# Rank and bias products in fp16, first expert rows ahead of three weight loads, row indices in a ring

## The chip, the cores and the metric

One core of a Trainium2 chip. The metric is the device time of one execution in microseconds (us), the median of the runs. The core has a matrix engine (PE), a vector engine (DVE), an activation engine (ACT), a general engine (POOL) and a queue engine (SP). Transfers are issued from SP, ACT and POOL. PE's clock is granted at one of two levels, 1.2 and 2.4 GHz; the profile shows it as 0.50 and 1.00.

## The reference

The input is `x` (32 sequences of 64 tokens, 256 features, float32). Four layers follow each other:

```python
# L0: adapter with one of 16 domain experts per sequence, residual, layer norm
hidden = gelu(x @ down_W.T + down_b)
hidden = hidden @ expert_W[idx].T + expert_b[idx] + domain_emb[idx]
x = layernorm(hidden @ up_W.T + up_b + x) * gamma + beta
# L1: attention (16 heads, bias and mask) with adaptive norm, then a feed-forward of 1024
# L2: rotation of feature pairs by theta and phi of the sequence
# L3: norms, a style per sequence, then a mixture of 8 experts, two per token
probs = softmax(h_flat @ router_w)
gates, idx = top_k(probs, 2)
gates = gates / gates.sum(-1, keepdims=True)
combine = zeros((N, 8)).at[arange(N)[:, None], idx].add(gates)
hid = relu(einsum('nd,edf->nef', h_flat, exp_w1) + exp_b1)
eout = einsum('nef,efd->ned', hid, exp_w2) + exp_b2
y = einsum('ned,ne->nd', eout, combine)
return x + y
```

## The kernel before, in words

The 2048 tokens go in four chunks of 512 through layers 0 to 2 and the routing of layer 3. The order of every engine's work is written out by hand, and semaphores join the engines. Chunk `c` of the second half overlaps with the first half of later chunks. Each chunk holds 4 groups (TT) of 128 tokens.

The routing of a chunk: `route` (PE, L1573) makes the logits, `choose` (DVE, L1119) finds the two experts and writes `picks`, `rank` (PE, L1588) multiplies `picks` by a triangular matrix `lower` and by `ones` to give each token its place among the tokens of its expert, `token_gates` (DVE, L1140) works out the two gates, `find_place` (DVE, L1128) turns ranks into row numbers, and `dispatch` (POOL, L565) scatters each token's row twice to `dispatched` in device memory, in a region per expert. A row holds the features as fp16 halves (high and low), the token's number, its first expert and its gate values. `confirm` (POOL, L577) waits until the scatter has landed and tells ACT (`rows_sent`).

The expert biases are added by token, apart from the experts: `turn_gates` (PE, L1599) transposes the gate matrix, `copy_gates` (DVE, L1165) copies it from PSUM to `gate_f`, `expert_biases` (PE, L1605) multiplies it by `moe_b2`, `accumulate` (DVE, L1169) adds the result to the residual stream as `x4b`, and `store` (ACT's queue, L740) writes it to the output and counts `x_stored`. In chunks 0 to 2, DVE's order is `choose`, `token_gates`, `find_place`, `copy_gates`, `fill_rows` (the low halves of the rows), `split_low` (the split of the expert weights into fp16 halves, L910; SP loads the next part into `stage` after it), norm2, `accumulate`. In the last chunk it is `choose`, `token_gates`, `fill_rows`, `find_place`, the plan of the expert loop (L1318 to L1345, which tile of 128 rows belongs to which expert), `copy_gates`, `accumulate`.

The expert loop handles 39 tiles of 128 rows, sorted by expert. The split weights of all 8 experts come from `w_split` to `w_moe` in SBUF, 2048 KB each: experts 0 to 4 early, experts 5 to 7 (L491) only once `x_stored` says that the last store has landed, since they lie over buffers of the chunks. On ACT's queue, after `store` and the loads of the plan's values to registers (L812), `load_rows` (L816) loads the rows of a tile into `xs`; tiles 0 and 1 first, each later tile as a buffer gets free. PE turns the rows (`turn_rows`, L1707), DVE copies them to `xs_f` and works out the gates of the tile (`rows_in`, L1353). A step on PE is the up products of tile n mixed with the down products of tile n-2, with the turn of the rows of tile n+1 in its middle. ACT applies the bias and relu (L825), DVE splits the result in halves (L1377), ACT and DVE scale the output (L835, L1371) into `ys`, and POOL adds it to the output by an indirect transfer with the tile's row numbers `ids` (`add_rows`, L620), one at a time.

Of the kernel before, what the change touches and what calls it, by code (L numbers as in the profile page):

```python
# [25 lines left out]
P = 128  # L26
# [6 lines left out]
E = 8  # L33
# [36 lines left out]
        ("sty_b1", SH // 2, 1), ("sty_b2", P, 2 * KD), ("moe_b1", P, E * KF), ("iota_e", P, E),  # L70
        ("iota_t", P, ENTRIES), ("tile_m", P, NT), ("region", P, E))

# [12 lines left out]
def build(nc, t, out):  # L85
    with ExitStack() as ctx:
# [82 lines left out]
        moe_b1 = col["moe_b1"].rearrange("p (e f) -> p e f", e=E)  # L169
        iota_e, iota_t, tile_m, region = (col[n] for n in ("iota_e", "iota_t", "tile_m", "region"))  # L170
        ints = sb("ints", [P, 3 * B + NT], I32)
        dom_i, time_i, sub_i, tok_id = (ints[:, 0:B], ints[:, B:2 * B], ints[:, 2 * B:3 * B], ints[:, 3 * B:])
# [10 lines left out]
        router = sb("router", [P, KD, E])  # L183
        moe_b2 = sb("moe_b2", [E, D])
        mask_u8 = sb("mask_u8", [P, NT, S], U8)
# [57 lines left out]
        gate = sb("gate", [P, TT, E])  # L243
        gate_f = sb("gate_f", [E, CT])

        ones = sb("ones", [P, P])
        first1 = first
        first2 = sb("first2", [P, TT])
        picks = sb("picks", [P, TT + 1, E])
        seen = sb("seen", [P, E])  # L250
# [36 lines left out]
        ident16 = sb("ident16", [P, P], F16)  # L287
        meta = sb("meta", [P, ENTRIES, 4])
        gates = sb("gates", [P, ENTRIES])
# [7 lines left out]
        ys_low = [x1_kept[:, j, D:2 * D] for j in range(2)]  # L297
        ids = [sb(f"ids{j}", [P, 1], U32) for j in range(2)]
        xs_dram = nc.dram_tensor("dispatched", (E * CAP + P, ROW), F32).ap()
# [43 lines left out]
        h3_ready = count("h3_ready", 1)  # L343
        logit_done, gap_ready, gap_exp = count("logit_done", 1), count("gap_ready", 1), count("gap_exp", 1)
        gate_ready, gate_turned, gate_f_ready = count("gate_ready", 1), count("gate_turned", 1), count("gate_f_ready", 1)
# [3 lines left out]
        second_step = count("second_step", 58)  # L349

# [41 lines left out]
        def _(sp):  # L392
# [96 lines left out]

            sp.wait_ge(x_stored.sem, x_stored.of(NCH, 0))  # L490
            load_weights(FIRST_HALF, E)  # L491
            sp.wait_ge(weights_in, 16 * E)
# [3 lines left out]
        def _(pool):  # L496
# [122 lines left out]

            def add_rows(n, j):  # L620


                pool.wait_ge(gates_ready, n + 1)
                pool.nop(nofuse=True)
                pool.tensor_copy(ids[j][:], meta[:, bass.ds(n, 1), 0].bitcast(U32)).then_inc(ids_ready, 1)  # L625
                pool.wait_ge(ids_ready, n + 1)
                pool.wait_ge(ys_ready, n + 3)
                pool.nop(nofuse=True)
                pool.indirect_dma_start(  # L629
                    out=out[:, :], out_offset=bass.IndirectOffsetOnAxis(ap=ids[j][:, 0:1], axis=0),  # L630
                    in_=ys[j], in_offset=None, bounds_check=N - 1, oob_is_err=False,
                    compute_op=ALU.add).then_inc(rows_out, 16)
                pool.wait_ge(rows_out, n * 16 + 16)
                pool.nop(nofuse=True)
                pool.sem_inc(added, 1)

            pool.sem_inc(added, 2)
            with pool.Fori(0, TILES // 2) as i:
                for j in range(2):
                    add_rows(i * 2 + j, j)  # L640
            if TILES % 2:
                add_rows(TILES - 1, 0)

# [234 lines left out]
        def _(dve):  # L878
# [17 lines left out]
            dve.wait_ge(early_in, N_EARLY)  # L896
            dve.tensor_copy(ident16[:], ident[:]).then_inc(zeroed, 1)
            dve.tensor_copy(next_row[:], region[:]).then_inc(zeroed, 1)
            step(dve.tensor_copy(dom_f[:], dom_i[:]))
# [8 lines left out]
            assert done[0] == SETUP_DOM  # L908
            dve.wait_ge(zeroed, 8)
            def split_low(c, q):  # L910
# [130 lines left out]
            def second_half(c):  # L1041
# [98 lines left out]
                def token_gates():  # L1140

                    dve.wait_ge(rows_sent.sem, rows_sent.of(c, 0))
                    dve.tensor_copy(disp[:, :, D].bitcast(I32), tok_id[:, bass.ds(c * TT, TT)])
                    dve.tensor_scalar(disp[:, :, D + 1], first1[:], 100.0, None, ALU.add)
                    dve.wait_ge(gap_exp.sem, gap_exp.of(c, 1))
                    vec(dve.tensor_scalar(gate_d[:], gap_e[:], 1.0, None, ALU.add))
                    vec(dve.reciprocal(gate1[:], gate_d[:]))
                    vec(dve.tensor_tensor(gate2[:], gap_e[:], gate1[:], ALU.mult))

                    vec(dve.tensor_scalar(disp[:, :, D + 2], gate2[:], 1.0 / W_SCALE, None, ALU.mult))  # L1150
                    dve.scalar_tensor_tensor(disp[:, :, D + 3], gate1[:], 1.0 / W_SCALE, disp[:, :, D + 2], ALU.mult,
                                             ALU.subtract).then_inc(disp_ready.sem, 1)
                    dve.tensor_tensor(gated1[:], hot1[:], wide(gate1), ALU.mult)
                    vec(dve.tensor_tensor(gated2[:], hot2[:], wide(gate2), ALU.mult))
                    dve.tensor_tensor(gate[:], gated1[:], gated2[:], ALU.add).then_inc(gate_ready.sem, 1)

# [20 lines left out]

# [174 lines left out]

            def rows_in(n, j):  # L1353
# [8 lines left out]
                dve.wait_ge(gate_step, n * 2 + 2)  # L1362
                dve.tensor_tensor(gates[:, bass.ds(n, 1)], gates[:, bass.ds(n, 1)], xs[j][:, D + 2:D + 3],
# [17 lines left out]

            dve.sem_inc(ys_ready, 2)
            rows_in(0, 0)
            rows_in(1, 1)
            for g in range(2):
                halves(0, 0, 0, g)
            rows_in(2, 0)
            for g in range(2):
                halves(1, 1, 1, g)
            with dve.Fori(0, TURNS) as i:  # L1390
                for j in range(STEPS):
                    rows_in(i * STEPS + j + 3, (j + 1) % 2)
                    halves(i * STEPS + j + 2, j % 2, (j + 2) % 3, 0)
                    outputs(i * STEPS + j, j % 2)
                    halves(i * STEPS + j + 2, j % 2, (j + 2) % 3, 1)
            for n in range(LEFT, TILES):
                rows_in(n + 1, (n + 1) % 2)
                halves(n, n % 2, n % 3, 0)
# [7 lines left out]
        def _(pe):  # L1406
# [198 lines left out]
            def expert_biases(c):  # L1605
                pe.wait_ge(gate_f_ready.sem, gate_f_ready.of(c, 1))
# [26 lines left out]
            domain_experts(0)  # L1633
            pe.wait_ge(zeroed, 8)
            up_projection(0)
# [229 lines left out]
```

## Time and profile before

| what | value |
|---|---|
| median of 3 runs | 761.92 us (759.7 to 762.53) |
| the profiled execution | 761.58 us |
| its span in the trace | 759.8 us |
| busy PE / DVE / POOL / ACT | 577.8 / 481.5 / 281.6 / 262.7 us |
| mean granted clock of PE | 0.857 |

The profile is of one execution. The span goes from its first to its last instruction; 1.8 us lie around it. A busy share is an average over stages with different limits, so the stages are read one by one. The chunks take the time to about 494 us, the passage to the expert loop lies from there to 511 us, the loop itself ends near 741 us.

### The profile page before, as it was taken

The page shows a single profiled execution, that of the slowest core. Times are in us where ns is not written, and L with a number is a line of the kernel's source. Part 1 is how long each engine was busy: PE and PEld are TensorE (multiplying, and loading weights), DVE is VectorE, ACT ScalarE, POOL GpSimd, SP SyncE. Part 2 cuts the span into 40 slices and gives each one's busy share as a digit, 9 for nine tenths or more (in the row PEclk, how much of TensorE's full clock was granted, in tenths as well). Part 3 has the DMA queues.
Part 4 walks back from the last instruction along what each step waited for, and adds up shares of the span by engine and source line. Part 5 has one row for each costly group of instructions (what it writes and reads, how often), then busy time and mean ns, then how long its engine had stood idle before and what let it go on. Part 6 is the DMA issues. An engine that isn't in the chain of part 4 may idle for free.

```text
span 759.8 us, 16208 instructions
## 1 busy us (share of the span) xinstructions
PE 577.8 (76%) x5068; PEld 433.1 (57%) x5069; DVE 481.5 (63%) x1306; ACT 262.7 (35%) x548; POOL 281.6 (37%) x200
## 2 busy tenths in 40 slices
PE   3528678995969978589384871439999999999992
PEld 1415375583754747438383361327777787777771
DVE  5674784899679996717966127714656565655661
ACT  1215534524344153243231401004444444444440
POOL 0831628077055480564705010300423333323332
PEclk9558599998888999779785795559999999999997
DMA  8622474133064321553205673256223222222220
GB/s 291 234 78 66 145 251 141 34 112 110 2 227 190 102 82 40 177 239 112 102 9 166 230 278 137 97 192 227 44 40 47 44 42 42 44 41 36 49 42 1
DMA packets 41144, 86.28 MB, mean 114 GB/s; under 512 B 7317, under 2 KB 31790, under 8 KB 37006
## 3 DMA queue, kind: packets, MB, share of 16 engines
q1 hardware_dynamic: 22896, 65.13, 24.5%
q0 software_dynamic: 7200, 8.60, 6.6%
q10 hardware_dynamic: 11006, 12.01, 5.3%
q8 instruction: 25, 0.41, 0.2%
q14 instruction: 17, 0.14, 0.1%
HBM read 57.18 MB, written 29.44 MB: 114 GB/s over the span
## 4 chain that ended last, share of the span: by engine, by line
PE 55%; DVE 21%; DMA 8%; issue 5%; ACT 3%; POOL 3%; ACTq 3%; POOLq 0%; SPq 0%; DVEq 0%
PE bank L1563 8%; PE bank L1732 7%; PE bank L1554 6%; PE bank L1721 4%; PE bank L1723 4%; PE bank L1722 4%; DMA out_x<-x_kept,ids 4%; DMA stage<-in_moe_w 4%; PE bank L1733 3%; PE bank L1451 2%; PE bank L1518 2%; PE bank L1534 2%; PE bank L1508 2%; DVE split L914 2%; PE bank L1490 2%
## 5 line engine op out<-in xcount | busy, mean ns | idle before, releaser
L1721 PE MATMUL bank<-xs_f,w_moe 128*128 128x128 f16 x624 | 124.1, 221 | 6.9 <-issue 5.5
L1723 PE MATMUL bank<-xs_f,w_moe 128*128 128x128 f16 x624 | 124.1, 221 | 0.0
L1722 PE MATMUL bank<-xs_f,w_moe 128*128 128x128 f16 x624 | 123.6, 221 | 0.0
L825 ACT ACTIVATE stage<-bank,cols 128x128 f32<-128x128 f32 x312 | 88.5, 377 | 95.9 <-PE bank L1723 83.2
L629 POOL DMA_INDIRECT out_x<-x_kept,ids x39 | 61.9, 1587 | 65.0 <-DVE x_kept L1371 34.9
L1721 PEld LDWEIGHTS bank<-xs_f,w_moe 128*128 x624 | 61.4, 98 | 43.1 <-issue 14.1
L1732 PE MATMUL bank<-w_moe,split 128*128 x208 | 78.7, 380 | 0.7
L573 POOL DMA_INDIRECT dispatched<-disp,slot x32 | 34.1, 1067 | 121.0 <-DVE disp L1160 56.7
L1554 PE MATMUL bank<-w_moe 128*128 128x512 f32 x128 | 63.1, 656 | 16.2 <-ACT w_moe L707 16.2
L1416 PE MATMUL bank<-mats,w_moe 128*128 128x128 f32 x96 | 19.9, 375 | 57.2 <-DVE w_moe L957 57.2
L1722 PEld LDWEIGHTS bank<-xs_f,w_moe 128*128 x624 | 61.6, 99 | 2.6
L1723 PEld LDWEIGHTS bank<-xs_f,w_moe 128*128 x624 | 61.4, 98 | 1.2 <-issue 0.2
L536 POOL TENSOR_TENSOR w_moe<-w_moe,sc_max 128x2048 f32<-128x2048 f32 x8 | 32.9, 4114 | 72.8 <-DVE sc_max L1029 72.8
L1563 PE MATMUL bank<-w,w_moe 128*128 128x256 f32 x256 | 57.9, 386 | 0.8 <-ACT w_moe L713 0.8
L625 POOL COPY ids<-meta 128x1 uint32 (+1 forms) x39 | 14.0, 360 | 116.0 <-DMA out_x<-x_kept,ids 99.5
L1733 PE MATMUL bank<-w_moe,split 128*128 x208 | 56.7, 273 | 0.0
L1554 PEld LDWEIGHTS bank<-w_moe 128*128 128x128 f32 x128 | 26.8, 212 | 50.7 <-issue 33.2
L657 ACT ACTIVATE split<-stage 128x2048 f16<-128x2048 f32 x16 | 30.5, 1907 | 70.9 <-DMA stage<-in_moe_w 54.6
L1563 PEld LDWEIGHTS bank<-w,w_moe 128*128 128x128 f32 x256 | 48.9, 193 | 8.8 <-ACT w_moe L713 1.6
L914 DVE SCALAR_TENSOR_TENSOR split<-stage,split 128x2048 f16<-128x2048 f32 x16 | 42.9, 2681 | 15.6 <-ACT split L657 15.6
L1416 PEld LDWEIGHTS bank<-mats,w_moe 128*128 128x128 f32 x96 | 15.9, 194 | 60.5 <-DVE w_moe L957 58.0
L1356 DVE COPY xs_f<-bank 128x512 f16<-128x512 f16 x40 | 16.9, 424 | 47.9 <-PE bank L1711 47.9
(242 smaller groups left out, 1275.2 us busy)
## 6 DMA issues: line engine op xcount, KB each, us to landing
stage<-in_moe_w SPq DMA_DIRECT2D x16, 1024.0 KB, 7.8
w_split<-split SPq DMA_DIRECT2D x16, 1024.0 KB, 5.0
w_moe<-w_split SPq DMA_DIRECT2D x8, 2048.0 KB, 8.2
w_moe<-in_bias SPq DMA_DIRECT2D x8, 1024.0 KB, 11.0
xs<-dispatched ACTq DMA_DIRECT2D x41, 130.0 KB, 2.1
w_moe<-in_x_f SPq DMA_DIRECT2D x4, 512.0 KB, 5.6
w_moe<-in_x_t SPq DMA_DIRECT2D x4, 512.0 KB, 5.1
out_x<-x4b ACTq DMA_DIRECT2D x4, 512.0 KB, 5.4
```

The source lines that it names most:

```text
L573: pool.indirect_dma_start(out=xs_dram[:, :], out_offset=bass.IndirectOffsetOnAxis(ap=slot[:, a, i:i + 1], axis=0), in_=disp[:, i, :], in_o ...
L629: pool.indirect_dma_start(out=out[:, :], out_offset=bass.IndirectOffsetOnAxis(ap=ids[j][:, 0:1], axis=0), in_=ys[j], in_offset=None, bound ...
L825: ins = act.activation(h32[j][:, f, :], bank[2 * j + g][:, P * (f % 4):P * (f % 4) + P], ACT.Relu, bias=moe_b1[:, bass.ds(e, 1), f], scale ...
L914: dve.scalar_tensor_tensor(low, part, W_SCALE, high, ALU.mult, ALU.subtract).then_inc(split_lo.sem, 1)
L1416: mm = pe.transpose(bank[first_bank + k][:, P * i:P * i + P], z[:, i, P * k:P * k + P], ident[:])
L1554: mm = pe.matmul(bank[4 + f % 2][:], w1[:, k, P * f:P * f + P], h_f[:, k, :], start=(k == 0), stop=(k == KD - 1))
L1563: mm = pe.matmul(bank[6 + i // 2][:, D * (i % 2):D * (i % 2) + D], ff[:, f, P * i:P * i + P], w2[:, f, :], start=(f == 0), stop=(f == KF - 1))
L1721: pe.matmul(o, hi, xs_f[j][:, k, :], start=(k == 0), stop=False)
L1722: pe.matmul(o, hi, xs_f[j][:, KD + k, :], start=False, stop=False)
L1723: mm = pe.matmul(o, lo, xs_f[j][:, k, :], start=False, stop=(k == KD - 1))
L1732: pe.matmul(o, h_hi[m][:, f, :], rows_of, start=(f == 0), stop=(f == KF - 1), skip_group_check=True)
L1733: mm = pe.matmul(o[:, 0:D], h_lo[m][:, f, :], rows_of[:, 0:D], start=False, stop=(f == KF - 1), skip_group_check=True)
```

## The change

- `rank`: `lower`, `ones` and `picks` become fp16 (their values are 0 and 1). `lower16` is made once by DVE.
- Biases: the gates are scaled by 256 and split into a high and a low fp16 part (`gate_parts`, 24 columns: high, high, low), by two more DVE operations in `token_gates`. `turn_gates` turns 24 fp16 columns per group. `moe_b2` is loaded three times below each other and made into `b2_parts` (fp16: high, low, high) by three DVE operations before the chunk loop. `expert_biases` is one fp16 product per group; `accumulate` divides by 256 squared as it adds.
- Rows: before SP issues the weights of experts 5 to 7, it waits for the first row load into each `xs` buffer.
- Indices: DVE copies the tile's row numbers from `xs` to a ring of 6 `ids` buffers in place of its copy to `meta`; POOL no longer copies them. POOL's loop body holds 6 tiles, not 2.

```diff
-        moe_b2 = sb("moe_b2", [E, D])
+        moe_b2 = sb("moe_b2", [3 * E, D])
+        b2_parts = sb("b2_parts", [3 * E, D], F16)
...
-        gate_f = sb("gate_f", [E, CT])
-
-        ones = sb("ones", [P, P])
+        gate_parts = sb("gate_parts", [P, TT, 3 * E], F16)
+        gate_f = sb("gate_f", [3 * E, CT], F16)
+
+        ones = sb("ones", [P, P], F16)
+        lower16 = sb("lower16", [P, P], F16)
...
-        picks = sb("picks", [P, TT + 1, E])
+        picks = sb("picks", [P, TT + 1, E], F16)
...
-        ids = [sb(f"ids{j}", [P, 1], U32) for j in range(2)]
+        ids = [sb(f"ids{j}", [P, 1], U32) for j in range(STEPS)]
...
             sp.wait_ge(x_stored.sem, x_stored.of(NCH, 0))
+            for j in range(2):
+                sp.wait_ge(xs_in[j], 16)
             load_weights(FIRST_HALF, E)
...
-            def add_rows(n, j):
-
-
-                pool.wait_ge(gates_ready, n + 1)
-                pool.nop(nofuse=True)
-                pool.tensor_copy(ids[j][:], meta[:, bass.ds(n, 1), 0].bitcast(U32)).then_inc(ids_ready, 1)
+            def add_rows(n, j, m):
+
                 pool.wait_ge(ids_ready, n + 1)
...
-            with pool.Fori(0, TILES // 2) as i:
-                for j in range(2):
-                    add_rows(i * 2 + j, j)
-            if TILES % 2:
-                add_rows(TILES - 1, 0)
+            with pool.Fori(0, TILES // STEPS) as i:
+                for m in range(STEPS):
+                    add_rows(i * STEPS + m, m % 2, m)
+            for n in range(TILES // STEPS * STEPS, TILES):
+                add_rows(n, n % 2, n % STEPS)
...
+            dve.tensor_copy(lower16[:], lower[:]).then_inc(zeroed, 1)
...
-                    dve.tensor_tensor(gate[:], gated1[:], gated2[:], ALU.add).then_inc(gate_ready.sem, 1)
+                    vec(dve.tensor_tensor(gate[:], gated1[:], gated2[:], ALU.add))
+                    hi = gate_parts[:, :, 0:2 * E].rearrange("p n (r e) -> p n r e", r=2)
+                    dve.tensor_scalar(hi, gate[:].unsqueeze(2).broadcast_to([P, TT, 2, E]), W_SCALE, None, ALU.mult
+                                      ).then_inc(gate_hi.sem, 1)
+                    dve.wait_ge(gate_hi.sem, gate_hi.of(c, 1))
+                    dve.scalar_tensor_tensor(gate_parts[:, :, 2 * E:], gate[:], W_SCALE, gate_parts[:, :, 0:E], ALU.mult,
+                                             ALU.subtract).then_inc(gate_ready.sem, 1)
...
-                    dve.tensor_copy(gate_f[:], bank[2][0:E, :]).then_inc(gate_f_ready.sem, 1)
+                    dve.tensor_copy(gate_f[:], bank[2][0:3 * E, 0:CT // 2].bitcast(F16)).then_inc(gate_f_ready.sem, 1)
...
-                        dve.tensor_tensor(x4b[:, 2 * g:2 * g + 2, :],
-                                          bank[2 + g][:].rearrange("p (n d) -> p n d", d=D),
-                                          x4[:, 2 * g:2 * g + 2, :], ALU.add).then_inc(acc_ready.sem, 1)
+                        dve.scalar_tensor_tensor(x4b[:, 2 * g:2 * g + 2, :],
+                                                 bank[2 + g][:].rearrange("p (n d) -> p n d", d=D), 1.0 / W_SCALE ** 2,
+                                                 x4[:, 2 * g:2 * g + 2, :], ALU.mult, ALU.add).then_inc(acc_ready.sem, 1)
...
+            dve.tensor_scalar(moe_b2[:], moe_b2[:], W_SCALE, None, ALU.mult).then_inc(b2_step, 1)
+            dve.wait_ge(b2_step, 1)
+            dve.tensor_copy(b2_parts[:], moe_b2[:]).then_inc(b2_step, 1)
+            dve.wait_ge(b2_step, 2)
+            dve.scalar_tensor_tensor(b2_parts[:], b2_parts[:], lo_rows[:, 0:1], moe_b2[:], ALU.mult, ALU.add
+                                     ).then_inc(b2_step, 1)
...
-                dve.tensor_copy(meta[:, bass.ds(n, 1), :].rearrange("p a w -> p (a w)").bitcast(U32),
-                                xs[j][:, D:ROW].bitcast(U32)).then_inc(gate_step, 1)
+                dve.tensor_copy(ids[m][:], xs[j][:, D:D + 1].bitcast(U32)).then_inc(ids_ready, 1)
...
-                pe.matmul(bank[0][:, 0:(TT + 1) * E], lower[:], picks[:].rearrange("p n e -> p (n e)"),
+                pe.matmul(bank[0][:, 0:(TT + 1) * E], lower16[:], picks[:].rearrange("p n e -> p (n e)"),
...
-                    mm = pe.transpose(bank[2][0:E, P * i:P * i + P], gate[:, i, :], ident[:])
+                    mm = pe.transpose(bank[2][0:3 * E, P // 2 * i:P // 2 * (i + 1)].bitcast(F16), gate_parts[:, i, :],
+                                      ident16[:])
...
-                    mm = pe.matmul(bank[2 + i // 2][:, D * (i % 2):D * (i % 2) + D], gate_f[:, P * i:P * i + P], moe_b2[:],
+                    mm = pe.matmul(bank[2 + i // 2][:, D * (i % 2):D * (i % 2) + D], gate_f[:, P * i:P * i + P], b2_parts[:],
```

## Rows read from the trace of the kernel before

**Rows 1.** The page: the granted clock in 40 slices, and the chain by engine

```profile
PEclk9558599998888999779785795559999999999997
...
PE 55%; DVE 21%; DMA 8%; issue 5%; ACT 3%; POOL 3%; ACTq 3%; POOLq 0%; SPq 0%; DVEq 0%
```

**Rows 2.** Busy us (x instructions) of each engine by stage, then clock and DMA

```profile
498.50:510.20 11.70, 0.00 (x0) 0.01 (x1) 0.00 (x0) 0.00 (x0) 0.00 (x0) 0.50 0.69 247
510.20:515.20 5.00, 4.58 (x42) 4.33 (x43) 1.58 (x8) 0.64 (x3) 0.22 (x1) 0.50 0.85 288
...
511.00:741.00 230.00, 222.43 (x2628) 174.46 (x2626) 137.86 (x351) 101.06 (x348) 70.64 (x72) 0.99 0.30 60
```

**Rows 3.** The chain of waits into the expert loop: start us, us, what

```profile
493.93 3.79 PE bank L1608 x8
497.75 0.70 DVE x4b L1174
498.47 0.38 ACTq L743
...
502.15 7.93 DMA xs<-dispatched
...
510.22 0.60 PE bank L1711 x4
```

**Rows 4.** DMA issues and landings in windows 494:495, 511:513 and 527:528

```profile
dispatched<-disp,slot POOLq DMA_INDIRECT x2, 2.5
...
xs<-dispatched ACTq DMA_DIRECT2D x1, 130.0 KB, 6.4
...
xs<-dispatched ACTq DMA_DIRECT2D x1, 130.0 KB, 2.1
```

**Rows 5.** Timeline of the queues: start us, from the first to the last issue

```profile
501.72 17.05 SPq L474 DMA_DIRECT2D w_moe<-w_split  x3
502.15 10.19 ACTq L819 DMA_DIRECT2D xs<-dispatched  x3
```

**Rows 6.** Timeline of the turn of tile 2's rows and its copy

```profile
520.23 0.39 PE L1711 MATMUL bank<-ident,xs 128*128 128x128 f16 x4
520.66 0.42 DVE L1356 COPY xs_f<-bank 128x512 f16<-128x512 f16 x1 [1.99 <-PE bank L1711]
```

**Rows 7.** Timeline of `place` in chunks 2 and 3, and the last scatter

```profile
402.21 0.19 DVE L1131 TENSOR_TENSOR place<-bank,next_row 128x32 f32<-128x32 f32 x1 [0.82 <-PE bank L1594]
...
483.77 0.18 DVE L1131 TENSOR_TENSOR place<-bank,next_row 128x32 f32<-128x32 f32 x1
...
494.51 0.96 POOL L573 DMA_INDIRECT dispatched<-disp,slot  x1 [0.30 <-issue]
```

**Rows 8.** The chain of waits in chunk 1

```profile
307.37 1.03 PE bank L1602 x4
...
308.42 0.68 DVE gate_f L1167
...
312.91 9.44 DMA stage<-in_moe_w
```

**Rows 9.** Timeline of DVE after norm2, of one output, and of POOL's last adds

```profile
131.29 0.68 DVE L968 TENSOR_TENSOR w_moe<-bank,add_o 64x512 f32<-64x512 f32 x1 [9.49 <-PE bank L1431]
...
740.51 0.48 DVE L1371 SCALAR_TENSOR_TENSOR x_kept<-bank,gates,x_kept 128x256 f32<-128x256 f32 x1 [0.75 <-ACT x_kept L835]
...
745.56 0.18 POOL L625 COPY ids<-meta 128x1 uint32 x1 [1.53 <-DMA out_x<-x_kept,ids]
...
750.79 1.57 POOL L629 DMA_INDIRECT out_x<-x_kept,ids  x1 [0.86 <-POOL ids L625]
```

**Rows 10.** Chain of waits: ACT's last load issue at the start, and two late adds

```profile
14.08 1.51 ACTq L739
...
742.45 2.75 DMA out_x<-x_kept,ids
...
746.65 2.73 DMA out_x<-x_kept,ids
```

More of the change, by code:

```diff
@@ L70 @@
         ("sty_b1", SH // 2, 1), ("sty_b2", P, 2 * KD), ("moe_b1", P, E * KF), ("iota_e", P, E),
-        ("iota_t", P, ENTRIES), ("tile_m", P, NT), ("region", P, E))
+        ("iota_t", P, ENTRIES), ("tile_m", P, NT), ("region", P, E), ("lo_rows", 3 * E, 1))
 class Count:
@@ L170, in build @@
         iota_e, iota_t, tile_m, region = (col[n] for n in ("iota_e", "iota_t", "tile_m", "region"))
+        lo_rows = col["lo_rows"]
         ints = sb("ints", [P, 3 * B + NT], I32)
@@ L287, in build @@
         ident16 = sb("ident16", [P, P], F16)
-        meta = sb("meta", [P, ENTRIES, 4])
         gates = sb("gates", [P, ENTRIES])
@@ L344, in build @@
         logit_done, gap_ready, gap_exp = count("logit_done", 1), count("gap_ready", 1), count("gap_exp", 1)
+        b2_step, gate_hi = sem("b2_step"), count("gate_hi", 1)
         gate_ready, gate_turned, gate_f_ready = count("gate_ready", 1), count("gate_turned", 1), count("gate_f_ready", 1)
@@ L348, in build @@
         adapter_step, attention_step = count("adapter_step", 24), count("attention_step", 2)
-        second_step = count("second_step", 58)
+        second_step = count("second_step", 59)
         picks_ready, rank_done = count("picks_ready", 1), count("rank_done", 1)
@@ L629, in add_rows @@
                 pool.indirect_dma_start(
-                    out=out[:, :], out_offset=bass.IndirectOffsetOnAxis(ap=ids[j][:, 0:1], axis=0),
+                    out=out[:, :], out_offset=bass.IndirectOffsetOnAxis(ap=ids[m][:, 0:1], axis=0),
                     in_=ys[j], in_offset=None, bounds_check=N - 1, oob_is_err=False,
@@ L908, in _ @@
             assert done[0] == SETUP_DOM
-            dve.wait_ge(zeroed, 8)
+            dve.wait_ge(zeroed, 9)
             def split_low(c, q):
@@ L1350, in _, with rows_in @@
             dve.wait_ge(w_out.sem, w_out.of(NCH, 0))
-            def rows_in(n, j):
+            def rows_in(n, j, m):
                 dve.wait_ge(turned, n + 1)
@@ L1357, in rows_in @@
                                 ).then_inc(xs_f_ready, 1)
-                dve.tensor_copy(meta[:, bass.ds(n, 1), :].rearrange("p a w -> p (a w)").bitcast(U32),
-                                xs[j][:, D:ROW].bitcast(U32)).then_inc(gate_step, 1)
+                dve.tensor_copy(ids[m][:], xs[j][:, D:D + 1].bitcast(U32)).then_inc(ids_ready, 1)
                 dve.tensor_scalar(gates[:, bass.ds(n, 1)], xs[j][:, D + 1:D + 2], tile_e[:, bass.ds(n, 1)],
                                   xs[j][:, D + 3:D + 4], ALU.is_equal, ALU.mult).then_inc(gate_step, 1)
-                dve.wait_ge(gate_step, n * 2 + 2)
+                dve.wait_ge(gate_step, n + 1)
                 dve.tensor_tensor(gates[:, bass.ds(n, 1)], gates[:, bass.ds(n, 1)], xs[j][:, D + 2:D + 3],
@@ L1382, in _ @@
             dve.sem_inc(ys_ready, 2)
-            rows_in(0, 0)
-            rows_in(1, 1)
+            rows_in(0, 0, 0)
+            rows_in(1, 1, 1)
             for g in range(2):
                 halves(0, 0, 0, g)
-            rows_in(2, 0)
+            rows_in(2, 0, 2)
             for g in range(2):
@@ L1391, in _ @@
                 for j in range(STEPS):
-                    rows_in(i * STEPS + j + 3, (j + 1) % 2)
+                    rows_in(i * STEPS + j + 3, (j + 1) % 2, (j + 3) % STEPS)
                     halves(i * STEPS + j + 2, j % 2, (j + 2) % 3, 0)
@@ L1396, in _ @@
             for n in range(LEFT, TILES):
-                rows_in(n + 1, (n + 1) % 2)
+                rows_in(n + 1, (n + 1) % 2, (n + 1) % STEPS)
                 halves(n, n % 2, n % 3, 0)
@@ L1601, in turn_gates @@
                 for i in range(TT):
-                    mm = pe.transpose(bank[2][0:E, P * i:P * i + P], gate[:, i, :], ident[:])
+                    mm = pe.transpose(bank[2][0:3 * E, P // 2 * i:P // 2 * (i + 1)].bitcast(F16), gate_parts[:, i, :],
+                                      ident16[:])
                 mm.then_inc(gate_turned.sem, 1)
             def expert_biases(c):
+                pe.wait_ge(b2_step, 3)
                 pe.wait_ge(gate_f_ready.sem, gate_f_ready.of(c, 1))
                 for i in range(TT):
-                    mm = pe.matmul(bank[2 + i // 2][:, D * (i % 2):D * (i % 2) + D], gate_f[:, P * i:P * i + P], moe_b2[:],
+                    mm = pe.matmul(bank[2 + i // 2][:, D * (i % 2):D * (i % 2) + D], gate_f[:, P * i:P * i + P], b2_parts[:],
                                    start=True, stop=True)
@@ L1633, in _ @@
             domain_experts(0)
-            pe.wait_ge(zeroed, 8)
+            pe.wait_ge(zeroed, 9)
             up_projection(0)
@@ L1832 @@
         "tile_m": every_lane(np.arange(NT) * P), "region": every_lane(np.arange(E) * CAP),
+        "lo_rows": -(np.arange(3 * E) // E == 1).astype(np.float32).reshape(3 * E, 1),
     }
@@ L1853 @@
         "hyp_w1": a["L3_cond_hyp_w1"], "sty_w2": a["L3_cond_sty_w2"], "router": a["L3_cond_router_w"],
-        "moe_w1": a["L3_cond_exp_w1"], "moe_w2": a["L3_cond_exp_w2"], "moe_b2": a["L3_cond_exp_b2"],
+        "moe_w1": a["L3_cond_exp_w1"], "moe_w2": a["L3_cond_exp_w2"], "moe_b2": np.concatenate([a["L3_cond_exp_b2"]] * 3, 0),
     }
```

## The prediction

> **What bounds the kernel.** I read the page first [rows 1]. Its chain of work gives PE 55%, DVE 21%, DMA 8%: no single engine sets the end, the bound changes from stage to stage. The busy times by stage [rows 2] show where. From 511 to 741 us, the expert loop, PE is busy 222.4 of 230 us at full clock (2.4 GHz): PE is the bound, and work taken off POOL, DVE or the queues inside that loop is worth nothing until the loop is over. From 498.5 to 510.2 us no compute engine works at all. So I took the chain of waits through this gap [rows 3] and read it backwards from the first turn of expert rows at 510.22: a row load issued at 502.15 that took 7.93 us, ACT's register loads behind the issue of the `x4b` store (498.47 to 502.15), the second `x4b` addition (497.75), the bias products (from 493.93, 3.79 us), and before these the copy of the gates and DVE's plan. Each link waits for the one before, so a microsecond out of any of them starts the expert loop a microsecond earlier.
>
> **Why that row load is slow.** SP issues the three weight loads of 2048 KB from 501.72 on, one after the other over 17.05 us, so some 8 us each; the row loads come 0.4 us later [rows 5]. Beside weights the first took 7.93 us and the third 6.4; one issued at 527.6, when the weights are in, took 2.1 [rows 3, 4]. SP starts the weights only when the `x4b` store has landed, so that store is not the company.
>
> **The change, part by part.**
>
> *Rows ahead of weights.* SP now waits for both first row loads before it issues experts 5 to 7. I take the load from 7.9 to 2.1 us: -5.8. Below I see no faster row; above stands the 6.4 of the third load, should something other than weights slow fresh rows (rival D). Behind SP's new wait stand only these three loads. In the time of before they ended near 527 us, and expert 5 of 8 comes past half of the 39 tiles, so their delay is free.
>
> *Biases in fp16, last chunk.* Before, from the products' start to the store's issue: 498.47 - 493.93 = 4.54 us [rows 3]. After, four fp16 products of 256 columns at half clock (1.2 GHz). Four fp16 transposes of 128 columns took 0.60 there [rows 3]; the first two products have the same columns in all, so I take 0.60 until the first half is ready. Then come two additions on DVE, 0.70 each before and now scalar_tensor_tensor; that form on 256 elements from PSUM takes 0.48 [rows 9], so I allow 0.72 for 512. In all 0.60 + 1.44 + 0.03 = 2.1: -2.45. Bounds: -2.7 (0.40 for the products, as at full clock [rows 6], and 0.70) and -1.7 (1.2 for the first half, 0.8 per addition).
>
> *Gates.* The copy of the turned gates took 0.68 us in fp32 [rows 8]; a copy of as many fp16 elements from PSUM takes 0.42 [rows 6]: -0.25. Against it stand two more dependent DVE operations in `token_gates`. One of this size takes 0.18 [rows 7], some 0.22 with its wait, and the drain after `gate` is new too: +0.47. `fill_rows`, `find_place` and the plan are queued behind them on DVE and shift by it. A faster `rank` gives nothing in this chunk: `place` at 483.77 shows no wait for PE [rows 7].
>
> Is something else last at ACT's row load, now issued 2.2 us sooner, at 499.9? ACT also waits until the scatter is confirmed. Its last piece is issued at 494.51 for 0.96 us and lands 2.5 us later [rows 4, 7]; shifted by 0.47, that is 498.4. Cover of 1.5 us; past it, each microsecond of lateness costs one.
>
> Sum at the start of the loop: -5.8 - 2.45 - 0.25 + 0.47 = -8.0 us.
>
> *The same edits in chunks 0 to 2.* There the chain runs from this DVE sequence through `split_low` into a load of `stage` of 9.44 us [rows 8], so DVE's delays count and PE's bias products, done beside that load, do not. Chunk 0 (a DVE sequence without waits): +0.47 - 0.25 = +0.2. Chunk 1: the copy waited for the turn of the gates (1.03 us from 307.37); in fp16 that lies behind `find_place`, which itself comes 0.47 later: about 0. Chunk 2: `place` waited 0.82 us for `rank` [rows 7]; five fp16 products, by the 0.60 of four, are done before DVE is, so the wait goes and the new steps fill half of it: -0.35, with the copy -0.6. Sum -0.3; bounds +1.4 (three times 0.47) and -1.5.
>
> *Preparation.* Three DVE operations for `b2_parts` (256 elements each, so at most 0.48 as the form above, 1.4 in all) stand before norm2 of chunk 0; DVE afterwards idles 9.49 us for PE [rows 9]: free, and 1.4 us without that cover. The load of `moe_b2` has 24 rows, not 8; its issue took 1.51 us on ACT's queue, in the chain that starts the kernel [rows 10]. I take +0.1, bounds 0 and +1.5 (double). One more small cast on DVE lies beside ACT's issues: 0.
>
> *Ids by DVE in a ring.* DVE's copy of 4 words becomes a copy of one: 0. POOL loses a wait, a copy and a register step per tile. In the loop PE is the bound: 0. At the end it counts, since POOL's last adds follow each other [rows 9, 10]: landing at 745.20 (742.45 + 2.75), copy at 745.56 for 0.19, issue at 746.65. That is 1.45 us; without the copy it is 1.26, without all that precedes it too 0.9; two of four steps before it fall away with it, so I take 1.0. The add two tiles before the last is then issued as long after its `ys` as now after the copy, 0.9 (740.51 + 0.48 = 740.99): 741.9, not 742.45. The next: 741.9 + 2.75 + 1.0 = 745.65. The last: 745.65 + 2.73 + 1.0 = 749.4, not 750.79: -1.4. Bounds -0.4 (copies alone, and POOL lagging as before) and -1.6.
>
> **Sum.** -8.0 - 0.3 + 0.1 - 1.4 = -9.6. The profiled execution took 761.58 us (its span 759.8, and 1.8 around it): 752.0. It is 0.3 under the median of three, 761.92, which is less than the runs differ; I say 752.
>
> **A rule of the skill at one place.** The rows say that a row load beside weights takes 6.4 to 7.9 us, not 2.1. The Trainium skill (DMA: Bandwidth & Descriptors, Queues, rings and completion order) says that each DMA engine turns between the queues that have work, a packet at a time. By it a row load does not stand behind whole weight loads; it pays one weight packet for each of its own. With that the trace agrees. By it the third and fourth row loads, which still meet weights, would gain nothing, and the sum stays.
>
> **Rivals.**
>
> A. *The third row load is late* (754 to 757). It still meets weights. Before, it was issued at 512.0 (three issues from 502.15, the last ends at 512.34) and its rows were turned at 520.23 [rows 5, 6]: 8.2 us of room, of which it took 6.4 and at most 7.9. Against: issue and need move together, so the room stays. For: the margin is 0.3 at worst. If it took 10 us, PE would stand 2 us, and if its clock fell, run 5 us at half speed as at the start [rows 2], 2.5 more. 0.12.
>
> B. *Another wait takes the place of the biases.* The scatter or the plan ends last at ACT, and -2.2 shrinks to 0: 754. Against: the 1.5 us of cover. 0.10.
>
> C. *The chunks move.* The granted clock there changes between half and full many times [rows 1]. PE now has less to do between them, and work of 1 to 3 us that runs at the other level than before moves the time by as much: 749 or 755. 0.13.
>
> D. *Not weights.* The row load stays slow for another reason; the load gains at most 7.9 - 6.4: 756.5 to 758. Against: 2.1 without weights. 0.05.
>
> E. *Slower*: PE's clock. The loop starts with 5 us at half clock [rows 2]. If after a stall as in A it stayed there, each tile would cost 5.9 us more (230 us over 39 tiles). The second such tile eats the 9.6; the third makes it slower, 765 or more. Against: once up, the clock stayed up through the loop. 0.04.
>
> The forecast as summed has 0.56, its own range is 750 to 754. With A to C the range is 748.5 to 757. Half a per cent, 3.8 us, is about what a measurement of this kernel can tell from no change, so faster means under 758.1. D lies at that bound. Faster 0.91, same 0.05, slower 0.04.
>
> **What would show it.** The first row load lands about 2 us after its issue, with the weights issued behind it; the bias products last about 1 us; the gap without compute before the loop shrinks from 11.7 us to some 6; the last adds on POOL stand about 1.0 us behind each landing; `place` of chunk 2 does not wait. The prediction is wrong where PE waits for rows at tile 2 or 3, where ACT's first row load waits for the scatter, or where the chunks shift by over 2 us.

## The result and the profile after

The changed kernel takes 754.59 us, median of 8 runs (751.12 to 760.74), against 761.64 us (759.66 to 762.64) beside it: ratio 0.9922, 95% interval 0.9899 to 0.9945. By the forecast's own bound (under 758.1 us) it is faster. It lies 2.6 us above the forecast of 752, inside the range with rivals A to C (748.5 to 757) and 0.6 above the forecast's own range (750 to 754). The unusual part is the scatter: 3.0 us before, 9.6 us after, from 10.5 us under the median of before to 0.9 us under it.

The profiled execution took 751.12 us (span 749.3), 0.9 us under the forecast. The page, the clock by slice and the chain by engine (against [rows 1]):

```profile
PEclk9559699999887998769976696559999999999997
...
PE 58%; DVE 23%; issue 8%; DMA 4%; POOL 3%; ACT 2%; ACTq 0%; SPq 0%; DVEq 0%; POOLq 0%
```

The DMA share of the chain has halved, 8% to 4%. Busy times by stage (against [rows 2]): the gap from the store's issue to the first up product, the first 5 us of the loop, the loop as far as 724.7 us.

```profile
494.57:502.20 7.63, 1.19 (x8) 0.69 (x8) 1.16 (x7) 0.00 (x0) 0.00 (x0) 0.50 0.37 121
502.20:507.20 5.00, 4.95 (x56) 4.69 (x56) 1.25 (x5) 1.62 (x6) 0.00 (x0) 0.68 0.99 343
502.20:724.70 222.50, 214.78 (x2548) 168.96 (x2549) 128.69 (x336) 97.67 (x337) 55.90 (x35) 0.99 0.33 70
```

The chain of waits into the loop (against [rows 3]):

```profile
494.57 0.38 ACTq L745
...
498.26 1.99 DMA xs<-dispatched
...
500.38 0.60 PE bank L1727 x4
501.00 0.42 DVE xs_f L1371
...
501.86 0.35 DVE xs_f L1371
502.21 0.28 PE bank L1737
```

The row load takes 1.99 us, not 7.93. It lands at 500.25. PE turns tile 0 and then tile 1 before its first up product, before as after. Before, the rows of both were in when PE began; now those of tile 1, issued 0.6 us behind, come in only then, and the first up product is at 502.21. From the load's issue to that product it is 3.95 us; before it was 9.5 (502.15 to 511.63). ACT's register loads between store and row load are as before, 3.3 us, and are now the largest link of the gap.

The passage before it, in the timeline (start us, us, engine, line, operation, idle time before in brackets):

```profile
481.00 0.20 DVE L1160 TENSOR_SCALAR gate_parts<-gate 128x64 f16<-128x64 f32 x1
...
481.23 0.19 DVE L1163 SCALAR_TENSOR_TENSOR gate_parts<-gate,gate_parts 128x32 f16<-128x32 f32 x1
...
482.54 0.18 DVE L1134 TENSOR_TENSOR place<-bank,next_row 128x32 f32<-128x32 f32 x1
...
492.01 0.40 DVE L1176 COPY gate_f<-bank 24x512 f16<-24x512 f16 x1
...
492.56 1.00 PE L1624 MATMUL bank<-b_parts,gate_f 24*128 24x256 f16 x4 [10.48 <-issue]
...
493.25 1.29 DVE L1183 SCALAR_TENSOR_TENSOR x4b<-bank,w_moe 128x512 f32<-128x512 f32 x2 [0.83 <-issue]
...
493.33 0.96 POOL L579 DMA_INDIRECT dispatched<-disp,slot  x1 [0.30 <-issue]
...
498.26 4.24 ACTq L821 DMA_DIRECT2D xs<-dispatched  x3
...
501.41 17.31 SPq L478 DMA_DIRECT2D w_moe<-w_split  x3
```

From products to the store's issue: 494.57 - 492.56 = 2.01 us, where it was 4.54. The gap in which no compute engine works, from the end of the additions (494.54) to the first turn (500.38), is 5.8 us, where it was 11.7 [rows 2] and some 6 were forecast. The last two rows answer to [rows 5]: the weights now start 3.15 us behind the row load, and they take the same 17 us. POOL's last adds, in the chain of waits (against [rows 9, 10]):

```profile
732.70 2.71 DMA out_x<-x_kept,ids
...
735.64 1.05 issue
736.69 2.71 DMA out_x<-x_kept,ids
...
739.63 0.72 issue
740.34 1.55 POOL out_x L631
```

The last landing is at 739.40, the last issue 0.94 us behind it (before: landing at 749.38, issue at 750.79, 1.41).

### The profile page after: what moved, and what is told of

Its sections match the earlier page's. It is cut to its first block, busy times and chain, and to the rows that moved or that the text cites. A ratio compares the mean times of both kernels' runs of the same rounds, so it can differ in the third digit from the quotient of the medians.

```text
span 749.3 us, 15939 instructions
## 1 busy us (share of the span) xinstructions
PE 562.9 (75%) x5032; PEld 420.8 (56%) x5033; DVE 479.5 (64%) x1318; ACT 262.3 (35%) x548; POOL 268.0 (36%) x161
## 4 chain that ended last, share of the span: by engine, by line
PE 58%; DVE 23%; issue 8%; DMA 4%; POOL 3%; ACT 2%; ACTq 0%; SPq 0%; DVEq 0%; POOLq 0%
PE bank L1748 9%; PE bank L1568 6%; PE bank L1577 6%; PE bank L1737 5%; PE bank L1739 5%; PE bank L1738 5%; PE bank L1749 4%; PE bank L1465 2%; DMA stage<-in_moe_w 2%; PE bank L1532 2%; PE bank L1548 2%; PE bank L1522 2%; DVE split L917 2%; DVE stats L950 1%; PE bank L1483 1%
## 5 line engine op out<-in xcount | busy, mean ns | idle before, releaser
L523 POOL TENSOR_TENSOR w_moe<-w_moe,mask_add 128x512 f32<-128x512 f32 x32 | 41.5, 1325 | 2.4 <-DMA w_moe<-in_bias 2.3
```

Of the source, the lines that this page charges most:

```text
L523: pool.tensor_tensor(sc[u][:, r], sc[u][:, r], mask_add[:, bass.ds(c * TT + 2 * u, 2), :].unsqueeze(2).broadcast_to([P, 2, 4, S]), ALU.add ...
```

## The experiments

Each ratio is against executions of the kernel before on the same chip; the chip differs from group to group, so kernels of different groups are compared by their ratios. A gain in us that is worked out from a ratio can differ from the difference of the medians by up to 1 us. By the traces, the span was split at these points: the last product of the last `route`, the issue of the last store, the issue of the first row load, the first and the last up product of the loop, and POOL's last add. "Loop" below is from the first to the last up product, "tail" from there to the last add; the last down products run 6 us into the tail.

### Once more, and the three parts alone

The first question was whether the scatter is real, and what each part is worth alone. `again` is the changed kernel unaltered.

> The changed kernel unchanged, a second time. Its profiled execution took 751.1 us, but its eight executions ran from 751 to 761 us, those of the kernel before only from 759.7 to 762.6. Theory 1 (the forecast, the four effects add up in every execution): the median is 751 to 753, and the spread is of the chip, not of the kernel. Theory 2 (something that an edit lets vary costs 0 to 9 us from execution to execution): the median is 753 to 757 again, the spread again near 10 us, and the mean granted clock is higher (0.88) in the longer executions.

Measured: 754.44 us (751.94 to 760.23, 11 runs), before 760.70 (759.29 to 764.52, 34 runs), ratio 0.9932 (0.9906 to 0.9958). The two sets of runs together: 11 of 19 lie at 751.1 to 754.7, 8 at 755.6 to 760.7.

```diff
# rows_only, on the kernel before
             sp.wait_ge(x_stored.sem, x_stored.of(NCH, 0))
+            for j in range(2):
+                sp.wait_ge(xs_in[j], 16)
             load_weights(FIRST_HALF, E)
```

> The kernel before with SP's two waits for the first row loads alone. By the forecast's own terms: row load 2.1 instead of 7.9 us, the rest as before: -5.8 us, 755.8, spread as before. If the third row load comes late in some executions (rival A), the loop's start shows a PE wait of 2 us or more and single executions lie above 758. If weights were not the company (rival D), -1.5 or less.

Measured: 761.51 us (759.12 to 764.83, 12 runs), ratio 1.0011 (0.9999 to 1.0023). The term of -5.8 us is not there. And yet the row load is fast (2.1 us from issue to landing) and the first up product comes 4.0 us after its issue, not 9.5. So the 5.5 us were gained and lost again inside the loop, which is 232.3 us long, not 227.5 (4.8 more). The timeline of this run shows where:

```profile
520.01 0.34 SPq L474 DMA_DIRECT2D w_moe<-w_split  x1
...
520.35 0.35 ACTq L821 DMA_DIRECT2D xs<-dispatched  x1
```

and its chain of waits:

```profile
514.48 0.44 ACTq L814
...
519.52 0.15 ACTq L814
...
520.35 8.00 DMA xs<-dispatched
...
528.39 0.40 PE bank L1713 x4
...
529.19 0.43 PE bank L1734
...
533.42 0.21 PE bank L1734
```

The row load of tile 4, the fifth, is issued 0.34 us behind the last weight load and takes 8.00 us. PE stands for 4.1 us, until 528.39, and then its products take 0.43 us, not 0.21: half clock until about 532.5. The chain also shows why this load has so little time: tile 4 is the first of ACT's loop body, and its row load is issued behind the register loads for the six tiles of that body (from 514.48 on). This execution is the fastest of the twelve (759.12 us). A won race would give about 757.5 (`rows_last_later` below), and none of the twelve is there; so it seems that all lost, though only this one is seen.

`ids_only` is the kernel before with the ring of `ids` and POOL's loop body of 6 tiles, nothing else of the change.

> The kernel before with the row numbers copied by DVE into a ring alone. Theory 1: the loop unchanged (PE bound), the tail -1.4 us, in the trace -1.0: 760.4, spread as before. Theory 2, if this edit is what varies: a spread of 5 us or more.

Measured: 760.71 us (758.42 to 762.05, 12 runs), ratio 0.9992 (0.9979 to 1.0005). `fp16_only` is the kernel before with the fp16 ranks, gates and biases, nothing else.

> The kernel before with the fp16 products of rank and biases alone. Theory 1: -2.2 us before the loop and -0.3 in the chunks, 759.2, spread as before; the first row load still takes 6 to 8 us, since the weights follow the store just as soon. Theory 2 for the chunks (rival C, PE's granted clock changes where PE has less to do): executions spread by 5 us or more, with mean clocks of 0.86 and 0.88 beside each other, and a median that is not under 760.

Measured: 760.17 us (757.50 to 763.05, 12 runs), ratio 0.9991 (0.9977 to 1.0005). In each trace the gain stands at its own place: the tail is 10.3 us with the ring and 11.7 before; from the last `route` to the store it is 18.6 with fp16 and 20.8 before. The timings give less than these traces: by the ratios 0.6 us for the ring and 0.7 for fp16, with intervals of 1 us either way, and by the medians 0.0 and 0.5.

### The last weight load behind the rows

Theory R after these runs: holding the weights back puts the last of them into a race with the row load of tile 4. Where the rows are issued first nothing happens, where the weights are first the loop loses 4 us or more. The rival is that the scatter belongs to the clock. The test takes the meeting away by holding the last weight load until the third row load into each buffer (tiles 4 and 5) has landed:

```diff
# last_later, on the changed kernel
-            load_weights(FIRST_HALF, E)
+            load_weights(FIRST_HALF, E - 1)
+            for j in range(2):
+                sp.wait_ge(xs_in[j], 48)
+            load_weights(E - 1, E)
```

> The changed kernel, with SP's issue of the last weight load (expert 7) put behind the row loads of tiles 4 and 5. Theory R (a race: the row load of tile 4 and the last weight load are issued within 0.3 us of each other; where the weights come first, the row load takes 8 us and PE stands 4 us or more and falls to half clock): no execution can lose it, so all lie at 751 to 754, median 752.5, spread under 4 us as before the change; tiles 2 and 3 still meet weights and still do not stall. Rival C (the spread comes from PE's clock in the chunks): nothing changes, median 754.5, spread 8 to 10 us.

Measured: 752.59 us (750.92 to 754.73, 4 runs), ratio 0.9870 (0.9848 to 0.9892). Its timeline, with the load of tiles 4 and 5 and then the weights:

```profile
521.78 0.35 ACTq L824 DMA_DIRECT2D xs<-dispatched  x1
...
523.93 0.34 ACTq L824 DMA_DIRECT2D xs<-dispatched  x1
...
526.17 0.36 SPq L478 DMA_DIRECT2D w_moe<-w_split  x1
```

Once more, since 4 runs are few:

> The kernel with the last weight load behind the row loads of tiles 4 and 5 is run once more, to have more than four of its executions. Theory R (in the changed kernel the row load of tile 4 meets the last weight load in some executions and loses 4 to 7 us there): the executions again lie within 4 us of each other, none above 756, median 751 to 753.5, ratio 0.984 to 0.990. Rival (the four executions seen were only lucky, and the scatter of the changed kernel is one of the clock): some of its executions lie at 757 to 761, and the median is near 754.5, ratio 0.992.

Measured: 752.08 us (750.45 to 754.09, 5 runs), ratio 0.9873 (0.9854 to 0.9893).

### Smaller weight transfers

The second theory to be told apart was on the price of the meeting. The Trainium skill (DMA: Bandwidth & Descriptors, Queues, rings and completion order) says that each DMA engine turns between the queues that have work, packet by packet. By it a row packet would pay for one weight packet, and smaller weight packets would make the meeting cheaper.

```diff
# quarters: on the changed kernel; old_quarters: on the kernel before
-                    sp.dma_start(w_moe[:, bass.ds(e * WE, WE)], ...).then_inc(weights_in, 16)
+                    for q in range(4):
+                        sp.dma_start(w_moe[:, bass.ds(e * WE + q * (WE // 4), WE // 4)],
+                                     w_dram[bass.ds(e, 1), :, q * (WE // 4):(q + 1) * (WE // 4)]
+                                     .rearrange("e p n -> p (e n)")).then_inc(weights_in, 16)
```

> The changed kernel, with every load of an expert's weights as four transfers of 512 KB (4 KB in a row of SBUF, not 16). If a row load beside weights pays one weight packet for each of its own (theory P), packets a quarter as long make the contended row load 3 to 4 us instead of 8, within the 8.2 us of room: no stall whichever comes first, median 752 to 753, spread under 4 us. If a row load waits for the amount of weights in front of it (rival), it stays at 6 to 8 us, and the race and the spread of 10 us stay.

Measured: 752.22 us (750.97 to 753.78, 4 runs), ratio 0.9879 (0.9859 to 0.9900). The loss is gone here too. But the issues moved as well: the row load of tile 4 is at 518.01 and the quarters of the last expert only from 520.67 on. What it meets is the end of the expert before, and PE turns its rows at 521.73 without a wait. So this run does not tell a cheaper meeting with the last expert from one that did not take place.

> The kernel before, with the weight loads in four transfers each and nothing else. Theory P: the first row load, still beside weights, takes 3 to 4 us, not 7.9: -4 us, 757. Its rival (amount in front): 7 to 8 us as before, 761.

Measured: 760.57 us (758.43 to 764.59, 12 runs), ratio 0.9982 (0.9967 to 0.9998). Here the rows do meet the weights. The first row load, issued at 500.80, was turned at 505.87, 5.1 us later, against 8.1 before: cheaper. The second, in the chain of waits:

```profile
501.46 7.20 DMA xs<-dispatched
...
508.70 0.62 PE bank L1715 x4
```

PE turns both before it starts, so its first product comes 9.1 us after the first issue, against 9.5. Packets a quarter as long made one load 3 us faster and the next hardly.

The packets in the traces show how the price comes about. In the kernel before, from the first row load's issue (502.15) to 506.3 the queues moved (queue: packets, MB, share; q1 carries the weights, q10 the rows)

```profile
q1 hardware_dynamic: 72, 1.18, 86.9%
```

and no row packet, and from 506.3 to 508.5

```profile
q1 hardware_dynamic: 56, 0.88, 94.0%
q10 hardware_dynamic: 53, 0.06, 7.1%
```

about one row packet for one weight packet. The other 235 row packets of the two loads went when the weights were nearly through. So the trace agrees with one for one in the second part only. In front of it stands a wait of 4.2 us in which 72 of the 128 weight packets pass; alone, a row load's first packet comes 1.0 us after its issue (527.61, 528.57). In `old_quarters` 80 small weight packets pass first, in 2.1 us. Then the first load's 128 row packets go by 505.3 and the second's only from there to 508.1, both beside weights that never run out: that is why the second gained so little. In the Trainium skill (DMA: Bandwidth & Descriptors, Queues, rings and completion order) a packet is typically 9 to 17 descriptors; whether the pieces that the profile counts here (16 KB, 128 to a weight load over 16 engines) are such packets is not shown, so the step from its rule to one for one was a reading of its own. What makes the first 43 to 80 weight packets pass alone (43 in `first_row_only`, 76 in `rows_only`) is not shown.

`quarters_later` joins both remedies.

> Both edits that removed the loss, together: the weights of an expert in four transfers and the last weight load behind the row loads of tiles 4 and 5. Theory R: the loss can be removed only once, so this is the same as either alone, 751 to 753.5, ratio 0.984 to 0.990, scatter under 4 us. Rival (smaller weight transfers bring something of their own, a faster row load at tiles 0 to 3): 1 to 2 us faster than the other kernel of this call, ratio 0.984 to 0.986.

Measured: 753.29 us (751.88 to 754.25, 5 runs), ratio 0.9888 (0.9870 to 0.9907), level with either alone, as it should be if there is one loss, which can be removed once.

### Without the rows, with one row, and the rows with the remedy

`no_rows_wait` is the changed kernel without SP's two waits.

> The changed kernel without SP's two waits: fp16 products and the ring of indices together. In the traces fp16 gave -2.2 us from the last logits to the store and the ring -1.4 in the tail; timed, each gave -0.5 with an interval of 1 us either way. Adding traces: 757.5. Adding timings: 759.7. Theory R says the executions spread no more than 5 us, since the weights begin 8 us before the first step and the last is issued 9 us before the row load of tile 4.

Measured: 758.56 us (757.40 to 759.18, 6 runs), ratio 0.9955 (0.9939 to 0.9971). fp16 and ring together are worth 3.4 us (2.2 to 4.6), as their traces say (2.2 + 1.4). `first_row_only` keeps only the first of the waits (`sp.wait_ge(xs_in[0], 16)`), which starts the weights 0.6 us sooner (2.55 us behind the first row load, not 3.15).

> The changed kernel with SP waiting for the first row load only, not for the second: the three weight loads begin some 0.6 us sooner against the loop. Theory R: the last weight load is then issued about 0.4 us before the row load of tile 4 in every execution, instead of within 0.3 us on either side. The race is always lost: PE waits about 4 us for the rows of tile 4 and runs a while at half clock, loop 232 us instead of 227.7, all executions at 756 to 761, median 758, spread under 5 us. Without a race (rival C), 0.6 us less waiting changes nothing: median 754.5, spread 8 to 10 us.

Measured: 759.00 us (755.01 to 760.77, 12 runs), ratio 0.9973 (0.9958 to 0.9987). So a shift of the weights by 0.6 us takes away the gain of the rows; this kernel is no faster than the one without any wait. Its timeline of the queues:

```profile
519.65 0.34 SPq L478 DMA_DIRECT2D w_moe<-w_split  x1
...
519.81 0.35 ACTq L820 DMA_DIRECT2D xs<-dispatched  x1
```

its chain of waits:

```profile
519.81 8.91 DMA xs<-dispatched
...
528.77 0.61 PE bank L1726 x4
...
532.57 0.43 PE bank L1747
...
534.87 0.21 PE bank L1747
```

and its windows over the stall and the 5 us after it:

```profile
519.00:529.00 10.00, 4.86 (x53) 3.30 (x51) 2.54 (x5) 3.65 (x13) 1.68 (x1) 0.93 0.74 252
528.00:533.00 5.00, 4.23 (x28) 3.23 (x29) 1.90 (x6) 0.00 (x0) 0.00 (x0) 0.50 0.03 6
```

The weights lead by 0.16 us (0.4 was expected), the row load takes 8.91 us, PE waits 5.0 and then works at 0.50 of its clock. The loop is 234.6 us long, 6.8 more than in the changed kernel's trace (227.8). `rows_last_later` is the kernel before with `rows_only` and `last_later`:

> The kernel before with the first rows ahead of the weights and the last weight load behind the row loads of tiles 4 and 5, without fp16 and ring. Theory R: the 5.3 us that the first row load gains, and which the rows edit alone lost again at tile 4, stay: loop 227.5, 755.5, against 761 for the rows edit alone. If that gain was lost in another way, 760 to 761.

Measured: 757.47 us (754.67 to 757.95, 6 runs), ratio 0.9946 (0.9928 to 0.9963), with a loop of 228.1 us. That is 2 us more than the 755.5 expected. The rows alone are worth 4.1 us (2.8 to 5.5) once the last weights are out of their way, and nothing without that (`rows_only`).

## Why the prediction was right, and what it missed

The parts came out about as forecast, and one loss came that the forecast did not have. That the median still fell inside the range is partly luck: the changed kernel stands on the edge of a race, and `first_row_only`, whose weights start 0.6 us sooner, lies at 759.0, outside the range and above the bound of 758.1.

**Rows ahead of weights** (forecast -5.8 at the loop's start): right in place, and in size -5.9 for the load itself. 0.4 us is given back because the second tile's rows now come in after the first's and both are turned before the first product: net 9.5 to 3.95, -5.5.

**"Behind SP's new wait stand only these three loads ... so their delay is free"**: this is the step that failed. It asked when the weights are needed and not whom they meet. The trace of the kernel before had both numbers. The last weight load was issued 9.2 us ahead of the row load of tile 4 and had landed (526.7) when that came; and the rows of tile 4 were turned 3.75 us after their issue:

```profile
518.43 0.34 SPq L474 DMA_DIRECT2D w_moe<-w_split  x1
...
527.61 0.35 ACTq L819 DMA_DIRECT2D xs<-dispatched  x1
...
531.36 0.39 PE L1711 MATMUL bank<-ident,xs 128*128 128x128 f16 x4
```

So a load of 8 us has room at tiles 2 and 3 (8.2 and 8.3 us from issue to turn) and none at tile 4. The change takes the first row load from behind the weights, so the loop starts sooner and the weights later, and the two issues fall together:

```profile
518.11 0.35 ACTq L821 DMA_DIRECT2D xs<-dispatched  x1
...
518.38 0.34 SPq L478 DMA_DIRECT2D w_moe<-w_split  x1
...
521.82 0.39 PE L1727 MATMUL bank<-ident,xs 128*128 128x128 f16 x4
```

In four traces (in brackets, the time since the issue of the first row load):

| trace | row load of tile 4 | last weight load | that row load |
|---|---|---|---|
| changed kernel | 518.11 (19.85) | 518.38 (20.12) | turned 3.7 us after issue, no wait |
| `again` | 521.46 (20.0) | 521.62 (20.2) | turned 3.7 us after issue, no wait |
| `first_row_only` | 519.81 (20.0) | 519.65 (19.8) | took 8.91 us, PE waited 5.0 |
| `rows_only` | 520.35 (20.0) | 520.01 (19.6) | took 8.00 us, PE waited 4.1 |

In these four a lead of 0.16 us either way decides. The issues of the two kinds come from two queues: the row load follows the pace of PE and ACT's register loads, nearly the same in all, the weights from the landing of the ones before, which varies more. The changed kernel sits on the edge.

Both profiled executions of the changed kernel are ones that won the race. That its slower executions are ones that lost it is inferred, not seen, from three things: the lost race is seen in two siblings, it costs 4.8 and 6.8 us of loop, and with the meeting taken away the 18 executions of `last_later`, `last_later_2`, `quarters` and `quarters_later` all lie at 750.45 to 754.73, whereas 8 of the 19 of the changed kernel lie above that. The median of the 19 is 754.4; without those 8 it is 752.9. So more than half of the 2.6 us between forecast and result is this race. The clock does not order them: of the eleven faster executions of the changed kernel seven had a mean granted clock of 0.85 to 0.86 and four of 0.88 to 0.89, of the eight slower ones three and five. Why `rows_only`, with the same two waits, has no execution that looks like a won race is not shown.

**Rival A** had the mechanism (late rows, then half clock), but at the third row load. It named the room there, 8.2 us, and that held: the third load took 7.5 us in `again` and PE did not wait. So the place where the rule of the Trainium skill (DMA: Bandwidth & Descriptors, Queues, rings and completion order) was weighed came out as written there: a row load that meets weights gains nothing (7.5 us, before 6.4). But "with that the trace agrees" said too much: of the 7.9 us of the first row load, 4.2 pass before its first packet, which one for one does not give. "Issue and need move together" holds for the row load and its need, but the weights do not move with them. That tile 3 or 4 can meet a weight load that was formerly ahead, and how much room it has there, was not asked. **Rival E**'s half clock came after each stall, and lasted 4 to 5.5 us, not the whole loop. **Rival D** did not come: with the weights behind it the load was fast.

**Biases and gates in fp16** (forecast -2.45 - 0.25 + 0.47 = -2.2): 18.6 against 20.8 us from the last `route` to the store, -2.2. The products took 1.00 us for all four, additions 0.65 each (forecast 0.72), the copy 0.40 (0.42), the two DVE steps 0.20 and 0.19. **Rival B** did not come: the last scatter is issued at 493.33 and, by [rows 4], lands about 2.5 us after its issue, at 495.8, against ACT's row load at 498.26. The cover was 2.4 us. The prediction reckoned 1.5, because it added the issue's own 0.96 us, which the 2.5 already hold (before: issued at 494.51, landed at 496.98).

**Tail** (forecast -1.4): 10.3 against 11.7, -1.4. The last step from landing to issue took 0.94, the one before 1.28; 1.0 was taken for both. Before they took 1.41 and 1.45.

**Chunks and preparation** (forecast -0.3 and +0.1): not to be resolved. The end of the last `route` lies anywhere from 475.8 to 479.6 us over the traces, with no order by kernel (kernel before 477.7, changed 476.0 and 479.2), so **rival C** can be neither seen nor excluded. `place` of chunk 2 shows no wait for PE, as said, 0.82 before:

```profile
402.27 0.18 DVE L1134 TENSOR_TENSOR place<-bank,next_row 128x32 f32<-128x32 f32 x1
```

**The sum**: -2.2, -5.5 and -1.4 are -9.1 of the forecast's -9.6. `last_later`, where no race interferes, measures 0.9870 and 0.9873, which is -9.7 to -9.9 us (by the medians -9.4).

**Open**: why `fp16_only` and `ids_only` give 0.7 and 0.6 us and 3.4 together (their intervals reach to 1.7 and 1.6, which holds the ring's 1.4 but not the 2.2 that the fp16 trace shows at its own place; in that trace the tail is 12.8 us, 1.1 more than before, of which 0.9 is one add that took 4.57 us and not 3.70); why weight packets pass alone before the first row packet; why all executions of `rows_only` seem to lose the race and less than half of those of the changed kernel; and what part of the difference of 3 to 4 us between the chunks of two executions is clock.

**The better version**: `last_later`, 752.6 and 752.1 us, ratio 0.987 (0.985 to 0.989), beats the kernel before by 9.4 us in the medians and 9.8 by the ratios. Its median is 2 us under that of the changed kernel, whose ratios are 0.992 and 0.993. Its scatter is 3.8 and 3.6 us in 4 and 5 executions, against 9.6 and 8.3 in 8 and 11.

## What to carry to other kernels

When a bulk transfer is moved back, list the small transfers that it will now meet, to the end of both streams, not only when its own data is needed; before and after the move, put the issue times side by side. For each small transfer read how long after its issue the data is used: the one with the least room decides, not the first. A kernel whose executions scatter wider after a change may have got a race between two queues: look for two issues a few tenths of a microsecond apart, and put an order in their place. A part that is tested alone can show nothing (`rows_only`) and yet carry half of the gain, when the loss that it causes can be removed.

## What the runs showed of the hardware

The first row load, 130 KB, took 2.0 to 2.2 us with no weights under way (changed kernel, `again`, `rows_only`, `first_row_only`). Issued behind a weight load of 2048 KB, which itself took 7.8 to 9.0 us, a row load landed about 0.2 us after it: that gave 8.9 us at 0.16 us behind, 8.0 at 0.34, 7.9 at 0.43 and 6.4 at 1.9 [rows 3, 4]. So its price was what was left of the weight load. For the first 2.1 to 4.4 us of it no row packet moved; after that about one for each weight packet. Issued 0.16 us ahead of the same weights it landed after 3.2 us (`again`) and was in time for a turn 3.7 us after its issue. What decided was who came first, by less than 0.2 us.

A stall of PE of 4.1 or 5.0 us was followed by 4 to 5.5 us at half clock (0.50 in the window above, products of 0.43 us, not 0.21); the loops were 0.7 and 1.8 us longer than the wait alone explains.
